# Layer-0 attention: where the score chunks and P.V stand between the transpose groups of a row tile

## The reference, cut to what matters

```python
attn = jnp.einsum('bhnd,bhmd->bhnm', qr, kr) + mask
out = jnp.einsum('bhnm,bhmd->bhnd', jax.nn.softmax(attn, axis=-1), vr)
```

## Time and profile before

| | us |
|---|---|
| median of 3 runs | 4024.16 (4020.73 to 4025.4) |
| the profiled execution's own time | 4022.89 |
| its span, first to last instruction | 4020.8 |
| PE busy | 3647.2 (91%) |
| DVE busy | 2767.1 (69%) |
| ACT busy | 2199.8 (55%) |
| POOL busy | 1445.0 (36%) |
| `layer0_core`, about | from 247 to 2880 |

### The profile page before, as it was taken

How to read it: one execution, slowest core, us unless ns; L and a number is a source line. 1 busy time by engine, 2 the same in 40 slices (tenths; PEclk the granted TensorE clock), 3 DMA queues, 4 the chain that set the end, 5 groups by cost and what they waited for, 6 DMA issues and landing times. The chain is left out here.

```text
span 4020.8 us, 98829 instructions
## 1 busy us (share of the span) xinstructions
PE 3647.2 (91%) x30782; PEld 2653.1 (66%) x30782; DVE 2767.1 (69%) x6801; ACT 2199.8 (55%) x3949; POOL 1445.0 (36%) x671
## 2 busy tenths in 40 slices
PE   7659999999999999999999999999769999999767
PEld 4436666666666666666666666666548787878655
DVE  6857777777777777777777777777556564644598
ACT  3236666666666666666666666666425444444433
POOL 2434444444444444444444444444310000000123
PEclk8879999999999999999999999999879999999978
DMA  5434124214223322322412421222132020000001
GB/s 160 154 91 117 60 88 116 84 60 122 82 85 83 98 82 89 91 85 82 121 60 85 119 83 61 90 82 84 53 114 75 14 74 14 26 1 0 27 13 36
DMA packets 122409, 307.36 MB, mean 76 GB/s; under 512 B 15609, under 2 KB 85292, under 8 KB 101548
## 3 DMA queue, kind: packets, MB, share of 16 engines
q1 hardware_dynamic: 122284, 305.78, 24.7%
HBM read 251.43 MB, written 54.31 MB: 76 GB/s over the span
## 5 line engine op out<-in xcount | busy, mean ns | idle before, releaser
L658 ACT ACTIVATE c_PT<-c_Tps 128x512 f32<-128x512 f32 (+1 forms) x2880 | 1568.1, 555 | 992.0 <-PE c_Tps L781 980.0
L720 DVE CUSTOM_DVE_ANT_0 c_S<-c_Sps,mask_tiles 128x768 f32<-128x768 f32 x1728 | 1602.8, 955 | 733.0 <-PE c_Sps L772 730.9
L639 POOL TENSOR_SCALAR c_S<-c_S,c_row_max 128x2304 f32<-128x2304 f32 x576 | 1261.5, 2190 | 1380.3 <-DVE c_row_max L731 1380.3
L781 PE MATMUL c_Tps<-ident,c_S 128*128 128x128 f32 x10368 | 1642.5, 278 | 74.4 <-ACT c_PT L658 7.4
L781 PEld LDWEIGHTS c_Tps<-ident,c_S 128*128 128x128 f32 x10368 | 1203.6, 140 | 552.7 <-ACT c_PT L658 235.3
L772 PE MATMUL c_Sps<-c_K,c_Q 96*128 (+1 forms) x3456 | 851.9, 327 | 72.8 <-DMA c_Q<-q_parts 39.7
L794 PE MATMUL c_Ops<-c_PT,c_V 128*32 128x256 f32 x10368 | 648.8, 383 | 0.5 <-ACT c_PT L658 0.5
L794 PEld LDWEIGHTS c_Ops<-c_PT,c_V 128*32 128x32 f32 x10368 | 292.7, 109 | 221.2 <-ACT c_PT L658 48.4
L1217 DVE TENSOR_SCALAR_CACHE_REDUCE l_S<-l_Sps 128x384 f32<-128x384 f32 x432 | 240.1, 557 | 270.9 <-PE l_Sps L1064 242.7
L772 PEld LDWEIGHTS c_Sps<-c_K,c_Q 96*128 96x128 bf16 x3456 | 338.8, 98 | 125.2 <-issue 46.4
L994 ACT ACTIVATE l_PT<-l_Tps 128x384 f32<-128x384 f32 x432 | 196.2, 491 | 395.1 <-PE l_Tps L1085 395.1
(11 more groups left out here) (209 smaller groups left out, 1911.6 us busy)
## 6 DMA issues: line engine op xcount, KB each, us to landing
mask_tiles<-in_mask SPq DMA_DIRECT2D x144, 1152.0 KB, 7.9
numerators<-c_O SPq DMA_DIRECT2D x288, 64.0 KB
l_num<-numerators SPq DMA_DIRECT2D x8, 2304.0 KB, 8.4
q_parts<-f_parts SPq DMA_DIRECT2D x12, 576.0 KB, 3.4
k_parts<-f_parts SPq DMA_DIRECT2D x12, 576.0 KB
c_Q<-q_parts SPq DMA_DIRECT2D x72, 96.0 KB
c_K<-k_parts SPq DMA_DIRECT2D x8, 864.0 KB, 8.7
c_vpad<-v_padded SPq DMA_DIRECT2D x8, 756.0 KB, 14.7
```

The lines of the kernel that those rows point to most:

```text
L639: pool.tensor_scalar(S[:, slot, :], S[:, slot, :], -1.0, row_max[:, slot:slot + 1], ALU.mult, ALU.add).then_inc(shifted, 1)
L658: act.activation(PT[:, b % 2, tiles.start:tiles.stop, cols(P, t)], Tps[:, (t + g) % T_SLOTS, 0:len(tiles) * P].rearrange("p (t q) -> p t q ...
L720: dve.tensor_tensor_reduce(out=S[:, r % ROW_SLOTS, cols(CH, c)].rearrange("p (k n) -> p k n", k=2), in0=Sps[:, n % S_SLOTS, :, 0:GW], in1= ...
L781: last = pe.transpose(Tps[:, (r + g) % T_SLOTS, cols(P, k)], S[:, r % ROW_SLOTS, cols(P, kt)], ident[:, :])
```

## The change

In each row tile the scores move back behind a later transpose group. Before, the order on PE is T0 S0 T1 V T2 S1 T3 S2 T4. After, in row tiles 0, 1, 2, 4, 5 and 6, it is T0 T1 V T2 S0 T3 S1 T4 S2; in row tiles 3 and 7, which have no V, it is T0 T1 S0 T2 S1 T3 S2 T4. Nothing is added or removed, and the order on DVE, ACT, POOL and SP is the same.

```diff
@@ -805,7 +805,6 @@
                     transposes(ip, r, 0)
-                    ahead(0)
                     transposes(ip, r, 1)
                     if r in (0, 1) and not start:
                         values(ip - 1, 1, r + 1)
@@ -813,11 +812,15 @@
                         values(ip, 0, r - 3)
                     if r in (2, 6):
                         values(ip, r // 4, 0)
+                    if r % 4 == 3:
+                        ahead(0)
                     transposes(ip, r, 2)
-                    ahead(1)
+                    ahead(0 if r % 4 < 3 else 1)
                     transposes(ip, r, 3)
-                    ahead(2)
+                    ahead(1 if r % 4 < 3 else 2)
                     transposes(ip, r, 4)
+                    if r % 4 < 3:
+                        ahead(2)
```

## The result

The changed kernel takes 4143.0 us (median of 4 runs, 4142.5 to 4148.0) against 4023.3 of the kernel before: the ratio is 1.030 (95% interval 1.028 to 1.032). The profiled execution took 4148.0, its span is 4145.8. It stands 5 above the median: the stages behind the one of the change, whose code is the same, took 1145.8 us against 1137.8 before, at a granted clock of 0.92 against 0.94. Slower was right, 4095 was too low, and 4143 lies outside the range of 4055 to 4118.

What follows compares the result with a forecast made beforehand. PE's order and its holds by ACT and DVE were taken to bound the kernel. Per pair 0.15 + 0.0 + 0.87 = +1.0 us, 71 us over 71 pairs, gave 4095 us, with a range of 4055 to 4118.

Steps and rivals of the forecast that it cites:

- The bound of ACT on T0: Row tiles with V: T0 can start no sooner than T3 + 1.29; the new order covers it, removing a 0.36 us hold.
- the bound of the slot on S2: Row tiles with V: S2 needs S0's slot, read by DVE, so starts at S0 + 1.65 or 1.74; hold 0.33 to 0.42.
- The V row tiles: Six per pair: period 4.88 or 4.97 against 4.89, together 0.15 to 0.2 us a pair more than before.
- the upper bound: All held S2 in register form and V rows restarting with 0.06: 0.3 and 0.36 us a pair more, 4141.
- Row tile 7: Row tile without V or a tap hold: 6.69 us from S2 to S0, costing 3.46, as before.
- Row tile 3, the step that failed: Chunk 0 waits behind the tap, S2 is held 1.23 instead of 0.61, T1 0.25 more: +0.87 us a pair.
- the second rival: A swap with no loss: V rows trade holds, row tile 3 loses nothing; 4024 to 4035 us, 6 in 100.
- The sum: Per pair 0.15 + 0.0 + 0.87 = +1.0 us; over 71 pairs 71 us, giving 4095.
- nothing passed a held S2: Denies the first rival: T0 and T1 run while S2 waits, giving 3870, or 3932 with row tile 3's loss; 4 in 100.
- The swap without loss: The second rival: pair 36.57 + 0 to 0.15 us, since chunk 0 in row tile 3 isn't as late or PE later.
- The third rival: Later S2 pushes DVE, DVE the next S0: each row tile 0.1 more, 43 us more, 4138; 5 in 100.
- The bound of +1.65 a pair and 4141: The upper bound from PE's restarts, set aside for 4118 as the upper end of the range.

Runs made afterwards that it cites:

- experiment 1: The changed kernel with TAP_ROWS (2, 4, 7) instead of (2, 5, 7), so no tap stands in front of chunk 0 of row tile 3: 4025.4 us.
- the third: Kernel before, reordered to T0 T1 S0 V T2 T3 S1 T4 S2 in every row tile: 3958.6 us; with TAP_ROWS (2, 4, 7) as well, 3890.7 us.
- experiment 4: The kernel before, with DVE issuing the tap straight behind the row maximum instead of behind the last chunk: 4257.4 us in one run.

## Why the prediction was wrong, and where it was right

- The bound of ACT on T0, the bound of the slot on S2, and that one takes the place of the other: right. S0 to S2 was worked out as 1.65 or 1.74 and is 1.66 or 1.75; the waits for the chunk moved as said (76 to 501), and the waits for ACT fell from 235 to 90 us.
- The V row tiles: 0.15 us a pair worked out, 0.3 measured. The missing 0.15 is the 0.05 to 0.06 by which the 2.5 row tiles with the register form are longer than worked out, most of it between T0 and V. I had put such a restart cost only into the upper bound.
- Row tile 7: 6.69 from S2 to S0 worked out, 6.68 measured (from the starts of PE's matmuls). Every second pair has 0.05 more there.
- Row tile 3, the step that failed: "The tap starts at 1.68, chunk 0 follows 1.33 later". It starts at 1.68 and chunk 0 follows 1.82 later. The 1.33 was taken from the earlier trace rows, where no shift ran beside the tap, and carried to an order in which the shift does. In the same text I worked out when the shift now runs, asked only whether it is in time for T0, and cost it at nothing; the second rival is turned down with the same words, "its times are fixed". Put there, the shift starts 0.64 + 0.88 + 0.32 = 1.84 behind S0 and ends at 4.04, and the tap starts at 1.66 + 1.68 = 3.34: an overlap of 0.70 could be read off the numbers on the page, and what an overlap of 0.52 does to a tap off the first tap of the trace of before. With it row tile 3 costs 0.87 + 0.48 = 1.35.
- The sum: 0.15 + 0.15 + 0.0 + 1.35 = 1.65 a pair, against 1.66 measured. 71 x 1.65 = 117 on 4022.9 gives 4140, and the runs' median is 4143.
- The rivals: nothing passed a held S2. In row tile 3 T4, whose slot was free by about 1801.8 (T2's start at 1800.47 and 1.29), starts at 1803.77, behind S2 at 1803.43; in row tile 0 the next T0, whose slot was free by about 1788.74 (T3's start at 1787.45 and 1.29), starts at 1789.21, behind S2 at 1788.87. The swap without loss fails in row tile 3. With the tap moved (experiment 1) the time is 4025, but the old order with the tap moved is at 4003, so the swap itself costs 23 us. The third rival, holds that build up from row tile to row tile, didn't occur: the periods are constant.
- The shape of the range was wrong too: its upper end was made of PE's restarts alone. No bound was given for a DVE instruction that moves beside another engine's. The bound of +1.65 a pair and 4141, which the prediction works out and then lowers to 4118, would have held nearly to the microsecond by luck: it adds 0.3 and 0.36 of restarts, and what came was about 0.15 of restarts and 0.48 of the tap.

## What to carry to other kernels

When an order is changed, list for every moved or delayed instruction what will run beside it on the other engines, not only who waits for it. A duration from the trace holds for the neighbours it had there. Two bounds of this kind (a slot behind ACT, a slot behind DVE) can be laid side by side as distances between starts, for every group and not only the one that is held now, and an order chosen that meets both. With a third bound overlooked that still gave 1.6%, and 3.3% with the tap moved as well. And the instruction that comes once in a few iterations (here the tap) belongs where the iteration has slack: moving it by one row tile was worth 18 us in the old order, 118 in the changed one and 68 in the third.

## What the runs showed of the hardware that was not expected

The tap, a DVE instruction with two SBUF inputs, and the shift, a GpSimd instruction that reads and writes SBUF, exclude each other, first come first served: the tap's 1.41 grows to 1.89 or 3.37, or the shift's 2.19 to 3.22. What is lost is the overlap less 0.1 to 0.2 us.

A wait of a score that stands on a register instruction costs PE more when it holds: 0.14 to 0.15 from the end of the read to the next matmul and 0.05 more behind it, against 0.06 where it stands on the weight load. A row tile's period in the changed kernel is 5.03 with the one and 4.89 with the other, same work.

In experiment 4 the score chunk S0 behind the long tap held PE for 2.74 us, and the granted clock fell behind it. The PE row and the window that begins with it:

```profile
1525.89 0.74 PE L772 MATMUL c_Sps<-c_K,c_Q 96*128 x2 [2.74 <-DVE c_part_max L720]
```
```profile
1525.80:1529.80 4.00, 3.91 (x30) 2.05 (x30) 1.75 (x5) 0.60 (x1) 1.82 (x1) 0.57 0.00 0
```

At 0.57, mostly the lower level of 1.2 GHz, the two score matmuls take 0.74 instead of 0.49 and V behind them 2.46 instead of 1.50. The stage mean of the granted clock is 0.97 instead of 1.00, and 77 of the 234 us of this version lie in the 47 pairs in which it fell. In 10 others a hold of the same length left it at 1.00, and so did the holds of 1.54 in the changed kernel.
